# A Macaron block on one core: first bodies and draining in an order of their own, and the next output weights' load in front of the kept half's write

## The reference

```python
x = x + 0.5 * ffn(layernorm(x), router_w, router_b, A, Bm)
x = x + attn(layernorm(x), wq_a, q_norm_w, wq_b, wkv_a, kv_norm_w, wkv_b, wo)
x = x + 0.5 * ffn(layernorm(x), router_w, router_b, A, Bm)

def ffn(x):                      # 8 experts, rank 16, top 2 of 8
    w = normalized top-2 of softmax(x @ router_w.T + router_b)
    h = einsum('nd,erd->ner', x, A) * w[:, :, None]
    return einsum('ner,eor->no', h, Bm) * 0.5

def attn(x):                     # q rank 384, kv rank 128, rope width 64
    q_nope, q_pe = split(rms_norm(x @ wq_a.T) @ wq_b.T)
    kv_c, k_pe = split(x @ wkv_a.T)
    k_nope, v = split(rms_norm(kv_c) @ wkv_b.T)
    scores = (q_nope . k_nope + rope(q_pe) . rope(k_pe)) / sqrt(192), causal
    return (softmax(scores) @ v) @ wo.T
```

## Time and profile before

| | |
|---|---|
| Median of 3 runs | 2231.49 us (2229.45 to 2236.15) |
| The profiled execution | 2233.13 us, of it a span of 2231.3 us |
| PE busy | 2142.0 us (96%) |
| PEld (weight loads beside it) | 1814.4 us (81%) |
| DVE busy | 1585.0 us (71%) |
| ACT busy | 1370.0 us (61%) |
| POOL busy | 1248.0 us (56%) |
| DMA | 258.01 MB, mean 116 GB/s |
| Mean granted TensorE clock | 0.989 |

### The profile page before, as it was taken

One profiled execution on the slowest core, in us unless ns is written; L12 is line 12 of the kernel. 1 busy time (PEld: TensorE's weight loads), 2 busy tenths in 40 slices (PEclk: granted clock), 3 DMA queues, 4 the chain that ended last, 5 costly groups with the idle time before them and its releaser, 6 DMA issues.

```text
span 2231.3 us, 44541 instructions
## 1 busy us (share of the span) xinstructions
PE 2142.0 (96%) x11548; PEld 1814.4 (81%) x11548; DVE 1585.0 (71%) x3415; ACT 1370.0 (61%) x3561; POOL 1248.0 (56%) x1643
## 2 busy tenths in 40 slices
PE   8978999999999999999899979999999999999998
PEld 7956888888888888888778958888888888888877
DVE  7646777776777667777777647777777777777777
ACT  6544666666666666666655446666666666666654
POOL 5324666676666666666554345555555555555543
PEclk9999999999999999999999989999999999999999
DMA  4024343333444444344424133333333333333331
GB/s 160 19 73 134 134 142 113 111 109 121 137 142 137 133 142 142 133 152 148 137 88 135 30 112 113 112 115 112 112 112 112 112 112 112 112 113 114 108 96 76
DMA packets 217104, 258.01 MB, mean 116 GB/s; under 512 B 145616, under 2 KB 174416, under 8 KB 214992
## 3 DMA queue, kind: packets, MB, share of 16 engines
q1 hardware_dynamic: 212432, 244.64, 35.3%
q10 hardware_dynamic: 4608, 12.58, 1.7%
HBM read 127.14 MB, written 79.69 MB: 93 GB/s over the span
## 4 chain that ended last, share of the span: by engine, by line
PE 62%; DMA 12%; POOL 8%; DVE 5%; issue 5%; ACT 4%; SPq 3%; POOLq 0%; ACTq 0%; DVEq 0%
PE ps L861 48%; DMA stage<-in_wo 8%; PE ps L940 4%; PE ps L1224 3%; PE ps L1168 2%; DMA arena<-arena 2%; SPq L756 1%; ACT stage L1695 1%; ACT arena L1386 1%; DVE xacc L2226 1%; DVE arena L1879 1%; POOL arena L2517 1%; PE ps L887 1%; PE ps L875 1%; POOL stage L2518 1%
## 5 line engine op out<-in xcount | busy, mean ns | idle before, releaser
L2226 DVE TENSOR_TENSOR xacc<-ps,xacc 128x512 f32<-128x512 f32 x896 | 602.6, 686 | 196.9 <-PE ps L861 183.1
L1879 DVE TENSOR_TENSOR arena<-ps,arena 128x512 fp32r<-128x512 f32 (+4 forms) x744 | 424.9, 576 | 250.4 <-ACT arena L1386 250.3
L861 PE MATMUL ps<-arena,extra 128*128 128x512 f32 x1920 | 523.0, 402 | 8.5 <-DVE xacc L2226 8.5
L1686 ACT ACTIVATE stage<-ps,negmax 128x128 f32<-128x128 f32 (+6 forms) x512 | 260.4, 509 | 339.9 <-DVE negmax L2205 333.3
L861 PE MATMUL ps<-zT,arena 128*128 128x512 f32 (+1 forms) x1746 | 450.3, 403 | 10.3 <-ACT stage L1386 7.0
L1386 ACT ACTIVATE arena<-ps 128x512 fp32r<-128x512 f32 (+4 forms) x744 | 369.1, 506 | 141.5 <-PE ps L861 60.5
L861 PEld LDWEIGHTS ps<-arena,extra 128*128 128x128 f32 x1920 | 342.6, 189 | 90.9 <-DVE xacc L2226 17.1
L861 PEld LDWEIGHTS ps<-zT,arena 128*128 128x128 f32 x1746 | 319.9, 191 | 80.1 <-ACT stage L1386 10.6
L2530 POOL TENSOR_TENSOR extra<-extra_plain,extra 128x256 fp32r<-128x256 f32 (+1 forms) x256 | 223.3, 875 | 198.6 <-ACT extra L1386 197.9
L861 PE MATMUL ps<-arena 128*128 128x512 f32 x960 | 264.2, 412 | 11.4 <-POOL arena L2530 5.2
L1695 ACT ACTIVATE stage<-stage,rrec 128x128 f32<-128x128 f32 (+6 forms) x512 | 237.6, 533 | 54.3 <-DVE rrec L2211 54.3
(11 more groups left out here) (129 smaller groups left out, 3127.2 us busy)
## 6 DMA issues: line engine op xcount, KB each, us to landing
kept_b<-arena SPq DMA_DIRECT2D x16, 3584.0 KB, 11.0
arena<-kept_b SPq DMA_DIRECT2D x112, 512.0 KB, 6.1
arena<-arena SPq DMA_DIRECT2D x128, 128.0 KB, 3.0
stage<-in_wo SPq DMA_DIRECT2D x16, 1024.0 KB, 13.0
stage<-stage SPq DMA_DIRECT2D x248, 64.0 KB, 2.0
extra<-arena SPq DMA_DIRECT2D x120, 128.0 KB, 3.0
kept_q<-arena SPq DMA_DIRECT2D x16, 768.0 KB, 4.1
arena<-kept_q ACTq DMA_DIRECT2D x32, 384.0 KB, 6.3
```

The source lines that it names most:

```text
L861: last = nc.tensor.matmul(dst, w, m, start=start and n == 0, stop=stop and n == len(passes) - 1, skip_group_check=skip)
L1686: nc.scalar.activation(prob[u][:, poff(u, i):poff(u, i) + w], bank_s(i)[:, 0:w], ACT.Exp, bias=negmax[:, k % 2, i:i + 1], accum_out=rowsum ...
L1879: return nc.vector.tensor_tensor(dst, src, part.bitcast(F32), ALU.subtract)
L2226: nc.vector.tensor_tensor(xs, bank_y(k, j), xs, ALU.add).then_inc(y_added, 1)
```

## The change

It has three parts, and no instruction that computes or moves data is added or removed.

**SP, pass 0.** `keep_b` loses its waits to a new `split_b`, and `load_wo(g + 1)` is issued between the two, so in front of the kept half's write, in the first body and in every body of the loop. `kept(g)` stays behind both.

**First bodies, both passes.** PE, ACT and DVE get an order of their own in pass 0 and in pass 1, where one order served both. On PE `q2` stands ahead of `values` of slot 0; in pass 0 the scores of slot 2 are mixed with `m2`, `m0`, `m1`, and output product 0 stands ahead of `pe0`, with `values` of slot 1 behind it; in pass 1 `values` of slot 1 stands ahead of `outputs(2, 0, 1)`, and `score(3, 3)` and `q1` ahead of `outputs(3, 0, 1)`. On ACT the two `split_a` of slot 2's sums go from behind `m3` and the transposes to behind the reads of `q3`, `m2` and `m0` (pass 0) or behind the first exponential of slot 2 (pass 1). `apart` gets bounds.

**Draining, both passes.** On PE the transposes of block 2 of the last slot stand ahead of output product 0, and product 0 of the last slot stands ahead of the waits for the half-layer's weights and its first product.

```diff
@@ SP
-            def keep_b(g):
+            def split_b(g):
                 sp.wait_ge(b_lo, 3 * g + 3)
                 settle(sp)
                 sp.wait_ge(t_lo, 4 * g + 4)
                 settle(sp)
+
+            def keep_b(g):
                 sp.dma_start(kept_b[bass.ds(g, 1)].rearrange("a p n -> p (a n)"),
                              arena(0, WB).bitcast(F32)).then_inc(wo_kept, 16)
...
-                    keep_b(g)
+                    split_b(g)
                     if not last:
                         load_wo(g + 1)
+                    keep_b(g)
                     kept(g)
@@ PE, first_body
-                fills("pf1")
+                fills("pf1", "q2")
                 values(slot_n(p, 0, 0), 0, True)
-                fills("q2")
                 turn(1, 0)
                 turn(1, 1)
...
                 if p == 0:
-                    values(slot_n(p, 0, 1), 1, False)
+                    fills("m3", "q3")
+                    turn(1, 2)
+                    fills("m2")
+                    turn(1, 3)
+                    score(2, 0)
                     fills("m0")
-                    score(2, 0)
                     score(2, 1)
                     fills("m1")
                     score(2, 2)
+                    outputs(2, 0)
                     score(2, 3)
                     fills("pe0")
-                    outputs(2, 0, 1)
+                    outputs(2, 1)
+                    values(slot_n(p, 0, 1), 1, False)
                     fills("w0")
                     outputs(2, 2, 3)
                     fills("w1")
                     outputs(2, 4, 5)
...
                 else:
+                    fills("q3")
+                    turn(1, 2)
+                    turn(1, 3)
                     score(2, 0)
                     score(2, 1)
                     fills("pe0")
                     score(2, 2)
+                    values(slot_n(p, 0, 1), 1, False)
                     outputs(2, 0, 1)
                     score(2, 3)
-                    outputs(2, 2, 3)
-                    outputs(2, 4, 5)
-                    values(slot_n(p, 0, 1), 1, False)
...
+                    turn(2, 2)
+                    score(3, 3)
+                    fills("q1")
+                    outputs(3, 0, 1)
+                    turn(2, 3)
@@ PE, drained
-                out_(0, 0, 1)
                 turn_probs(n, 3, 2, False)
-                out_(0, 2, 3)
+                out_(0, 0, 1, 2, 3)
...
                 turn_ffn(s, 1)
+                out_(1, 0)
                 pe.wait_ge(ra_hi, s + 1)
                 pe.wait_ge(ra_lo, s + 1)
                 up(0)
-                out_(1, 0, 1)
+                out_(1, 1, 2, 3)
                 turn_ffn(s, 2)
-                out_(1, 2, 3)
@@ ACT, first_body
-                fills("m3")
-                split_a(unit_n(p, 0, 2), 1)
-                turn(1, 2)
-                turn(1, 3)
-                split_a(unit_n(p, 0, 2), 2)
-                fills("q3", "m2", "m0")
...
+                    fills("m3")
+                    turn(1, 0)
+                    turn(1, 1)
+                    fills("q3")
+                    turn(1, 2)
+                    fills("m2")
+                    turn(1, 3)
+                    apart(p, 0, 2, 0, 1)
+                    fills("m0")
                     split_b(0, B11, first=True)
-                apart(p, 0, 2)
-                exps(p, 0, 2, 0)
-                fills("m1" if p == 0 else "pe0")
-                exps(p, 0, 2, 1)
-                if p == 0:
+                    split_a(unit_n(p, 0, 2), 1)
+                    exps(p, 0, 2, 0)
+                    apart(p, 0, 2, 1)
+                    split_a(unit_n(p, 0, 2), 2)
+                    fills("m1")
+                    exps(p, 0, 2, 1)
...
+                    exps(p, 0, 2, 3)
                     fills("pe0")
+                    norms(p, 0, 2)
```

More of the change, by code:

```diff
@@ L1100, in first_body @@
                     outputs(2, 4, 5)
-                else:
+                    score(3, 0)
+                    outputs(2, 6)
+                    score(3, 1)
+                    turn(2, 0)
+                    turn(2, 1)
+                    fills("q0")
+                    score(3, 2)
+                    turn(2, 2)
+                    outputs(3, 0, 1)
+                    score(3, 3)
+                    outputs(3, 2, 3)
+                    turn(2, 3)
+                    fills("q1")
+                    outputs(3, 4, 5)
+                    values(slot_n(p, 0, 2), 2, False)
+                    outputs(3, 6)
+                else:
+                    fills("q3")
+                    turn(1, 2)
+                    turn(1, 3)
                     score(2, 0)
@@ L1105, in first_body @@
                     score(2, 2)
+                    values(slot_n(p, 0, 1), 1, False)
                     outputs(2, 0, 1)
                     score(2, 3)
[L1108 to L1126 removed]
+                    outputs(2, 2, 3, 4, 5)
+                    score(3, 0)
+                    outputs(2, 6)
+                    score(3, 1)
+                    turn(2, 0)
+                    turn(2, 1)
+                    fills("q0")
+                    score(3, 2)
+                    turn(2, 2)
+                    score(3, 3)
+                    fills("q1")
+                    outputs(3, 0, 1)
+                    turn(2, 3)
+                    outputs(3, 2, 3)
+                    outputs(3, 4, 5)
+                    values(slot_n(p, 0, 2), 2, False)
+                    outputs(3, 6)
             def fill(p, g, name, ev):
@@ L1611, in first_body @@
[L1611 to L1625 removed]
+                    fills("w0", "w1")
@@ new lines, in first_body @@
+                    valued(slot_n(p, 0, 1), y_n(p, 0, 2) + 6)
+                    exps(p, 0, 3, 0)
+                    turn(2, 0)
+                    exps(p, 0, 3, 1)
+                    turn(2, 1)
+                    split_a(unit_n(p, 0, 3), 1)
+                    fills("q0")
+                    split_a(unit_n(p, 0, 3), 2)
+                    turn(2, 2)
+                    exps(p, 0, 3, 2)
+                    exps(p, 0, 3, 3)
+                    turn(2, 3)
+                    norms(p, 0, 3)
@@ new lines, in first_body @@
+                    fills("q1")
+                    valued(slot_n(p, 0, 2))
+                else:
+                    fills("q2")
+                    valued(slot_n(p, 0, 0))
+                    norms(p, 0, 1, 2, 3)
+                    turn(1, 0)
+                    norms(p, 0, 1, 3)
+                    turn(1, 1)
+                    fills("q3")
+                    turn(1, 2)
+                    turn(1, 3)
+                    q_weights_back(1, 0)
+                    q_weights_back(1, 1)
+                    apart(p, 0, 2, 0, 1)
+                    exps(p, 0, 2, 0)
+                    split_a(unit_n(p, 0, 2), 1)
+                    apart(p, 0, 2, 1)
+                    fills("pe0")
+                    split_a(unit_n(p, 0, 2), 2)
+                    exps(p, 0, 2, 1)
+                    exps(p, 0, 2, 2)
+                    exps(p, 0, 2, 3)
+                    norms(p, 0, 2)
+                    valued(slot_n(p, 0, 1), y_n(p, 0, 2) + 6)
+                    exps(p, 0, 3, 0)
+                    turn(2, 0)
+                    exps(p, 0, 3, 1)
+                    turn(2, 1)
+                    fills("q0")
+                    split_a(unit_n(p, 0, 3), 1)
+                    turn(2, 2)
+                    split_a(unit_n(p, 0, 3), 2)
+                    exps(p, 0, 3, 2)
+                    exps(p, 0, 3, 3)
+                    turn(2, 3)
+                    fills("q1")
+                    norms(p, 0, 3, 0, 3)
+                    valued(slot_n(p, 0, 2), whole=False)
+                    norms(p, 0, 3, 3)
+                    split_a(unit_n(p, 0, 4), 0)
@@ L1671, in read_fill, with apart @@
                 hi(dst, src).then_inc(q_act, 1)
-            def apart(p, g, k):
-                for i in range(NS):
+            def apart(p, g, k, first=0, end=NS):
+                for i in range(first, end):
                     w = keys_of(k % 2, i)
@@ L2110, in first_body @@
                 maxi(1, 0)
-                tokens(n)
-                maxi(1, 1)
-                inverses(p, 0, 0)
+                if p == 0:
+                    maxi(1, 1)
+                    inverses(p, 0, 0)
+                    tokens(n)
+                else:
+                    inverses(p, 0, 0)
+                    tokens(n)
+                    maxi(1, 1)
                 turn(0, 0)
@@ L2151, in first_body @@
                     adds(2, 5)
+                    maxi(3, 0)
+                    adds(2, 6)
+                    maxi(3, 1)
+                    turn(2, 0)
+                    turn(2, 1)
+                    fills("q0")
+                    maxi(3, 2)
+                    turn(2, 2)
+                    adds(3, 0, 1)
+                    maxi(3, 3)
+                    adds(3, 2, 3)
+                    turn(2, 3)
```

(5 more changed lines are left out.)

130 lines of the change are left out of this document (49 added, 81 removed).

## The result

| | before | changed |
|---|---|---|
| Median | 2230.87 us (5 runs, 2229.45 to 2236.15) | 2255.74 us (5 runs, 2248.29 to 2256.32) |
| Ratio to before | | 1.0100 (95% interval 1.008 to 1.0121) |
| Profiled execution, of it the span | 2233.13, 2231.3 us | 2255.74, 2253.9 us |
| Mean granted TensorE clock | 0.989 | 0.986 |

I had forecast 2207 us, with 2193 to 2222 as the range. The kernel went the other way, by the path of the third rival (2244.7 us, chance 0.08), and 11 us beyond its time.

A forecast was written before the change was run, and what follows sets the result against it. PE, busy 2142.0 of 2231.3 us, was taken as nearly full, with holes in the first bodies and drainings. The terms -16.5 - 11 - 2 + 5 = -24.5 us gave 2207.0 us against the median of 2231.49, range 2193 to 2222.

The forecast's parts named there:

- the third rival: Loop of pass 0: the write's delay isn't absorbed, 3.05 us in each of 14 bodies, +42.7, 2244.7 us; chance 0.08.
- First body, pass 0: ACT's reads ahead of its wait for POOL's sum let `score(3, 0)` start at about 168.2, not 184.08: -16.5 us.
- First body, pass 1: The 9.24 us hole goes, PE is held by POOL's sums alone, `score(3, 0)` at 1320.8: -11 us.
- The sign of being wrong that I had put down: First bodies: DVE or POOL holding PE for more than 3 us at one place would show the forecast wrong.
- The sign for the loop: Pass 0: the body's period changing by more than 1 us would show the forecast wrong.
- Draining: Both passes: moved transposes and a product fill PE's waits for POOL's sums: -2 us for both (-0.5 to -5).
- The loop: Pass 0: `m0`'s 0.39 us wait goes, but the later write delays swap, rotation and output product 0: +5 us (-5.5 to +12).
- the two don't overlap: Loop of pass 0: DMA engines idle between write's end and load's first packets, so no overlap; the +5 rests on it.
- Rival 1: Loop of pass 0: write overlaps the load's tail, slip under the 2.9 us slack, -5.5, whole 2196.5 us; chance 0.13.
- or 0.85: Loop of pass 0: new PE wait per body, 0.5 us, or 0.85 if the swap moves queue behind the write's last packets.
- The second rival: First bodies win a third, -9 of 27.5, as waits come back elsewhere; with the loop's +5, 2227.5 us; chance 0.17.
- the fourth: Loop of pass 0: change does nothing, another wait sets `m0`; 2202 us, inside the range, within the forecast's chance of 0.62.

The follow-up runs named there:

- rest_alone: The changed kernel with SP's issues in the order of before (kept half's write, then load), new first bodies and draining kept: 2203.37 us, ratio 0.9872 to before.
- first0: The kernel before with the new first body of pass 0 alone: 2219.59 us, ratio 0.9945.
- first1: The kernel before with the new first body of pass 1 alone: 2222.47 us, ratio 0.996.
- drains: The kernel before with the new order of PE in the two drainings alone: 2227.64 us, ratio 0.9982.
- load_early: The changed kernel with the loop's load moved ahead of the stacking moves, first body in the order of before: 2199.86 us, ratio 0.9855 to before.
- kept_later: The changed kernel, but SP waits for the write's end only behind the next body's first swap: 2199.98 us, ratio 0.9856 to before.

## Why the prediction was wrong

**What bounds the kernel, and where the gains are: right.** The holes in the first bodies and the drainings were the right place; `rest_alone` took 28.0 us out of them, where my sum had 29.5.

**First body, pass 0: right in mechanism, 2.6 us too much.** I had -16.5, `first0` measured -13.9, the stretch in the trace -13.7 or -14.3. The changed kernel's PE:

```profile
147.76 1.51 PE L1190 MATMUL ps<-stage 128*128 128x512 f32 x2 [2.18 <-DMA stage<-in_wo]
...
161.27 0.97 PE L865 MATMUL ps<-arena 128*128 128x512 f32 x3 [0.62 <-DVE arena L1949]
...
164.78 3.62 PE L865 MATMUL ps<-zT,arena 128*128 128x512 f32 x9 [1.37 <-DVE arena L1949]
...
175.89 0.60 PE L865 MATMUL ps<-keyT,arena 128*128 128x320 f32 x3
```

This trace runs 2.6 us late by its start, so product 0 begins at 158.6 on the clock of before, where I had 156.3, and `score(3, 0)` at 173.3, where I had 168.2 (before: 184.08). The low part that product 0 was to wait for came from POOL at 156.0, 0.6 us late, as late as the DMA that I took as unmoved (148.66, so 146.06 instead of 145.46); the rest is the new first fill in line, `m3`, which waits 2.18 us for its weights because it is reached earlier, DVE's low parts, and the low clock, which I had put at 3 us and half of it in the sum. In the windows, against the earlier trace rows, PE waits 6.1 of 50 us instead of 16.0 of 63, and the clock is 0.90 instead of 0.86; in pass 1 it is 6.5 of 43 instead of 14.0 of 54.

```profile
142.00:192.00 50.00, 43.89 (x190) 33.21 (x189) 30.29 (x60) 28.28 (x72) 20.90 (x25) 0.90 0.36 92
1329.00:1372.00 43.00, 36.48 (x170) 28.97 (x169) 22.38 (x49) 22.01 (x59) 19.40 (x25) 0.92 0.39 112
```

**First body, pass 1: right.** -11 forecast, -11.0 in `first1`, -10.4 in the trace. As put down, PE is held by POOL's sum alone, and by more than I thought since it is there early:

```profile
1349.32 2.90 PE L865 MATMUL ps<-arena 128*128 128x512 f32 x6 [4.87 <-POOL arena L2621]
...
1356.37 0.60 PE L865 MATMUL ps<-keyT,arena 128*128 128x320 f32 x3
```

With the offset of 34.8 us between the traces, the score stands at 1321.6, where I had 1320.8. The sign of being wrong that I had put down, a wait for POOL or DVE of over 3 us at one place, did come, and the time held all the same: PE now only reaches the wait earlier. (The sign for the loop, a period changed by over 1 us, came too, with 3.2.)

**Draining: the term was too small.** -2 forecast (-0.5 to -5), -4.7 measured. I took half of the 1.3 us per pass that the moved work fills, and hardly anything for the clock, which seems the larger part: the granted clock is 0.82 from 1110 to 1137 us before, and 1.00 from 1110 to 1136 in `drains`, and 27 x 0.18 is 4.9 us at most. The hole of 2.20 us is now two short ones of 0.94 and 0.65 us, and the window behind it has the full clock, where the earlier trace rows shows six matmuls in 2.55 us:

```profile
1154.52 0.63 PE L1246 MATMUL ps<-ident,stage 128*128 128x128 f32 x4 [0.94 <-DVE arena L1949]
1155.80 1.65 PE L865 MATMUL ps<-arena 128*128 128x512 f32 x6 [0.65 <-POOL arena L2621]
```

**The loop: the chain was right, the size of the slip wrong, and with it the sign.** The prediction named the path link by link: the write lands late, SP's swap slips, POOL's rotation slips, and output product 0 waits. The step that failed is "the write, now behind it, ends at about 453.0 instead of 449.95, 3.05 us later". In this body it was 5.36 us. The sum had some 4 us of queue for the load, and by that alone the slip would have been 4 and over the slack; I let the pair of transfers end when the pair had ended before. And 4 was itself too little, because I read a row wrongly. Windows of the two traces (clock, DMA share and GB/s are the last three columns), first of before, then of the changed kernel, each from the first issue of the group on:

```profile
438.90:440.00 1.10, 1.10 (x6) 0.88 (x6) 1.06 (x4) 0.27 (x1) 0.76 (x1) 1.00 1.02 417
...
447.00:448.00 1.00, 1.00 (x9) 0.95 (x8) 0.88 (x4) 0.90 (x3) 0.49 (x2) 1.00 1.84 459
448.00:449.00 1.00, 1.00 (x6) 0.78 (x6) 0.97 (x4) 0.84 (x3) 0.65 (x2) 1.00 0.00 0
```

```profile
442.70:444.00 1.30, 1.30 (x7) 1.06 (x6) 1.26 (x4) 0.38 (x1) 0.86 (x1) 1.00 0.11 32
...
457.00:458.00 1.00, 1.00 (x7) 0.76 (x7) 1.00 (x2) 0.00 (x0) 1.00 (x2) 1.00 0.20 86
```

A share of 1.84 is more than the engines have: the view counts a packet wholly in the window in which it starts. The write goes in 128 packets of 28 KB, of 1.1 us each, the last sixteen of 1.6 to 2.1 us; these start by 447.51 and end at 449.55. So the 0.00 of the earlier trace rows was no idle queue, and my reason for "the two don't overlap" was none. In the changed kernel the last three of the write's packets start in the window from 457 to 458 and end by 458.75. The packets' own times in the two bodies, in us from the first issue of the group:

| | before | changed |
|---|---|---|
| load's packets | 10.09 to 13.50 | 1.01 to 7.54 |
| write's packets | 0.87 to 10.62 | 5.53 to 16.02 |
| write landed, for SP | 11.00 | 16.36 |

Of the 5.36 us, 4.66 are the later start of the write's packets, and 0.74 that they are more spread: the first sixteen start over 1.1 us (448.26 to 449.36; before, within 0.15 us), and the last sixteen over 1.7. The time from the last packet's end to the landing is 0.4 and 0.3 us, nothing new. What I had wrong is the load: behind the write it takes 3.4 us from first to last packet, and at the head of an idle queue 6.5. There eleven of its first sixteen packets of 4 KB take 0.9 to 1.46 us each; behind the write the first sixteen take 0.16 us each. In `load_early`, at the head too but with the write far off, it takes 4.2 us. Why the start is so slow stays open.

By the rule that I weighed there, of the Trainium skill, DMA: Bandwidth & Descriptors, section "Two DMAs through the same engine are not ordered", the two should overlap. They do: the write's first packet starts 2.0 us before the load's last one ends. But over these 2.0 us load and write together fill the engines' time about once (0.9 to 1.0), so the trace shows no time won by it. Rival 1's time didn't come, but my row was no evidence against it.

The second failed step is "or 0.85": the new wait was 2.24 us, and the low clock, for which this sum had no term, came behind it. Its price can be read off the changed kernel itself, since not every body has it. Two bodies, as windows:

```profile
443.90:508.60 64.70, 61.61 (x308) 50.53 (x307) 43.45 (x95) 39.47 (x107) 39.92 (x46) 0.97 0.39 122
508.60:571.05 62.45, 59.89 (x308) 49.48 (x307) 43.41 (x95) 39.48 (x107) 39.92 (x46) 1.00 0.41 127
```

Both have the hole, 2.24 and 2.10 us, and the same work. One runs at 0.97 and takes 64.7 us, the other at 1.00 and takes 62.45. So per body 2.2 us of hole less the gain of about 0.4 at `m0`, and in nine of twelve bodies some 2 us for the clock: 1.8 + 0.75 x 2 = 3.3, where the period shows 3.2. Why three of the bodies kept the full clock isn't shown. Body 14 cost more, 66.22 us against 60.81, with a hole of 3.99 us for DVE's addition; I had +1.4 and +0.9 for the last two bodies.

**The rivals.** The third had the right path and the right sign, but its price of +42.7 us was near by luck: it took the whole of a slip of 3.05 us per body, as if nothing were absorbed. What happened was a slip of 5.36, less a slack that held, plus the low clock: 3.2. The point from which it decides, 2.6 us per body, was passed by 0.6. With a slack of 2.9 us against a slip of 3.05, read to the tenth from one row each, a chance of 0.08 was too low: the sum stood at the edge of a cliff. The second rival, first bodies worth a third, was wrong, and so were the first and the fourth: `m0`'s wait for the load did go, and only 2.7 us in 7 waits for ACT came in its place.

## What to carry to other kernels

When two transfers on one queue change places, cost the new pair from its own parts: start, packets, landing. The time that a transfer takes behind another need not be its time at the head of an idle queue (3.4 against 6.5 us here), and a share of 0.00 in a short window is no idle time where one packet is longer than the window: the window before it tells. Look first for who waits on the completion of the one that goes behind, and what is queued behind that wait; where a forecast leaves slack and slip within a few tenths, the chance belongs on both sides. And a long transfer that nobody needs soon costs little where it stands, if the wait for its end is put where its end is needed: that one move (`kept_later`) was worth 56 us here.

## What the runs showed of the hardware that I had not expected

- A write of 3584 KB takes 10.1 us to land when the loads went 9.5 us ahead of it, 11.0 us when they are issued right behind it (its last sixteen packets then take 1.6 to 2.1 us instead of 1.1), and 15.0 us when 1152 KB of loads are issued 1.15 and 0.57 us ahead of it. Halving the larger load took 2.46 of 5.36 us off the delay.
- The same 1152 KB of loads take 3.4 us from first to last packet behind the write, 4.2 us at the head of the queue with the write far behind, and 6.2 us there with the write right behind (medians of twelve bodies). The first packet starts 0.87 us after the issue for the write and 1.0 us for the load; the landing is seen 0.4 us after the last packet's end.
- A hole of some 2.2 us on PE was followed by the low clock in nine of twelve bodies and not in three, for a difference of about 2.2 us per body; with a hole of 0.28 us the body took 60.6 us.
